# Four graph layers on one core: VectorE reads PSUM for one operand, two banks are held longer, and the order tables are replaced

## The reference

```python
x = _layernorm(x + _L0_gnn_ref(x, adj, ...))   # attention, 12 heads of 32, masked by adj, beta * adj added
x = _layernorm(x + _L1_gnn_ref(x, adj, ...))   # two digraph convolutions
x = _layernorm(x + _L2_gnn_ref(x, adj, ...))   # two more, with softmax of h h^T and triangles
x = _layernorm(x + _L3_gnn_ref(x, adj, ...))   # attention with adj as an added bias, output projection
```

```python
u_left = einsum('bih,bjh->bij', h, h @ W_left.T) / temper
u_right = einsum('bih,bjh->bij', h, h @ W_right.T) / temper
u = u_left * upper_triangle_with_diagonal(adj) + u_right * transposed(upper_triangle(adj))
d = exp(u) * adj
ctx = (d / (d.sum(axis=2) + 1e-10)) @ (h @ W_lin.T + b_lin)
h = relu((ctx - mean) / (std + 1e-3) * ln_a + ln_b)
```

## Time and profile before

| | |
|---|---|
| median of 3 executions | 2729.16 us (2726.61 to 2732.68) |
| the profiled execution | 2730.39 us, span 2728.5 us |
| PE busy | 2582.3 us, 95% |
| POOL busy | 2117.1 us, 78% |
| DVE busy | 2077.7 us, 76% |
| ACT busy | 2046.5 us, 75% |
| mean granted clock of TensorE | 0.986 of full speed |

### The profile page before, as it was taken

The page is one execution under the profiler, slowest core; times in us unless marked ns, Lnnn a source line. Parts: engine busy times, 40 slices in busy tenths (PEclk is TensorE's granted clock), DMA queues, the critical chain, the costliest instruction groups (busy, mean ns, idle before and its releaser), DMA issues.

```text
span 2728.5 us, 90881 instructions
## 1 busy us (share of the span) xinstructions
PE 2582.3 (95%) x33728; PEld 1930.4 (71%) x33728; DVE 2077.7 (76%) x7848; ACT 2046.5 (75%) x5716; POOL 2117.1 (78%) x3211
## 2 busy tenths in 40 slices
PE   5899999999999999999999999999999999999995
PEld 4667777776777777777777777777777777777763
DVE  6677877777877777777777777777787777887774
ACT  6667777777777777777777777777777777787775
POOL 6577878778778788778787788888787787887774
PEclk9899999999999999999999999999999999999997
DMA  7734544445444544444454454444454544454433
GB/s 182 164 62 78 90 86 83 91 84 93 81 87 80 91 91 80 90 91 80 87 94 80 88 93 80 90 91 79 88 94 84 86 88 79 85 96 82 78 61 74
DMA packets 809952, 243.18 MB, mean 89 GB/s; under 512 B 768688, under 2 KB 808752, under 8 KB 809520
## 3 DMA queue, kind: packets, MB, share of 16 engines
q1 hardware_dynamic: 801056, 222.42, 45.5%
q10 hardware_dynamic: 8464, 14.94, 1.8%
HBM read 35.92 MB, written 12.58 MB: 18 GB/s over the span
## 4 chain that ended last, share of the span: by engine, by line
PE 45%; POOL 18%; DVE 16%; ACT 7%; DMA 6%; issue 6%; SPq 1%; DVEq 0%; POOLq 0%; ACTq 0%
PE bank L921 7%; PE bank L923 6%; PE bank L922 6%; PE bank L912 5%; PE bank L913 5%; PE bank L914 5%; DMA region<-region 5%; POOL region L717 3%; DVE region L1091 3%; POOL ab L733 3%; PE bank L995 3%; ACT region L832 2%; POOL region L706 2%; PE bank L951 2%; POOL region L733 2%
## 5 line engine op out<-in xcount | busy, mean ns | idle before, releaser
L912 PE MATMUL bank<-region,w_hi 128*128 128x128 f16 x3960 | 686.0, 220 | 35.0 <-DMA region<-region 25.0
L913 PE MATMUL bank<-region,w_hi 128*128 128x128 f16 x3960 | 685.6, 220 | 0.0
L914 PE MATMUL bank<-region,w_lo 128*128 128x128 f16 x3960 | 685.4, 220 | 0.0
L921 PE MATMUL bank<-w_hi,region 128*128 128x384 f16 x1815 | 593.9, 327 | 11.4 <-DMA region<-region 6.1
L923 PE MATMUL bank<-w_hi,region 128*128 128x384 f16 x1815 | 593.2, 327 | 0.0
L922 PE MATMUL bank<-w_lo,region 128*128 128x384 f16 x1815 | 593.1, 327 | 0.0
L717 POOL TENSOR_TENSOR region<-region 128x512 f16<-128x512 f32 x330 | 385.2, 1167 | 220.6 <-ACT region L838 219.2
L832 ACT ACTIVATE region<-region,small 128x128 f32<-128x128 f32 x1320 | 419.8, 390 | 133.1 <-DVE small L1091 73.2
L912 PEld LDWEIGHTS bank<-region,w_hi 128*128 128x128 f16 x3960 | 390.0, 98 | 63.3 <-issue 26.4
L1091 DVE CUSTOM_DVE_ANT_0 region<-bank,mask 128x128 f32<-128x128 f32 x1320 | 304.4, 285 | 134.5 <-PE bank L951 123.2
L913 PEld LDWEIGHTS bank<-region,w_hi 128*128 128x128 f16 x3960 | 389.9, 98 | 23.8 <-issue 16.5
(11 more groups left out here) (229 smaller groups left out, 7795.8 us busy)
## 6 DMA issues: line engine op xcount, KB each, us to landing
region<-region SPq DMA_TRANSPOSE x715, 3.1
last_unit<-w_dram ACTq DMA_DIRECT2D x19, 576.0 KB, 6.0
x<-x_dram SPq DMA_DIRECT2D x55, 192.0 KB, 2.5
out_dram<-region SPq DMA_DIRECT2D x55, 192.0 KB, 2.2
adj<-adj_dram SPq DMA_DIRECT2D x55, 64.0 KB, 2.3
mask<-adj_t_dram SPq DMA_DIRECT2D x55, 64.0 KB, 2.0
rows<-rows_dram ACTq DMA_DIRECT2D x5, 576.0 KB, 4.3
last_unit<-last_unit SPq DMA_TRANSPOSE x117, 3.1
```

The lines of the kernel that those rows point to most:

```text
L912: pe.matmul(dst, lhsT=w_hi[:, w, k, cols], rhs=t_hi[u][:, k, :], start=(k == 0), stop=False)
L913: pe.matmul(dst, lhsT=w_hi[:, w, k, cols], rhs=t_lo[u][:, k, :], start=False, stop=False)
L914: last = pe.matmul(dst, lhsT=w_lo[:, w, k, cols], rhs=t_hi[u][:, k, :], start=False, stop=(k == DT - 1))
L921: pe.matmul(dst, lhsT=t_hi[u][:, k, :], rhs=w_hi[:, w, k, :], start=(k == 0), stop=False)
```

## The change

The arithmetic is the same, but for where intermediate values lie:

- `divide` writes the reciprocals into a free part of the bank of `attend` 2 (k = 0) or `attend` 5 (k = 1), and the division reads them there. For k = 0 the result also goes into that bank, over its first 384 columns, and `residual` 0 reads it there. For k = 1 the reciprocal comes first and the three small instructions after it; one of their results goes into the bank too.
- `READ_BY` names `residual` 0 as the last reader of `attend` 2's bank and `divide` 1 as that of `attend` 5's, in place of ACT's copy. PE's next product in that bank waits for them.
- `u_gcn` is three instructions of 128 columns in place of one of 256 and one of 128: left half times mask into SBUF, right half times mask into its own place in the bank, and the sum of the two. The denominator of the first two inner norms goes into the last column of `mix`'s bank.
- All wanted times of `PARTS`, all of `SHIFTED`, and `PERIOD` are new. The estimates are the same but for those shown, and so are the parts and what they follow.

```diff
-PERIOD = 20.1080
+PERIOD = 20.0000
 SHIFTED = {
-    0: (-214.647, -123.076, -82.970, -144.420, -205.803, -198.625, -397.860, -243.257),
-    1: (2.746, -8.453, 4.931, -1.139, 6.274, 8.107, -14.342, 6.813),
+    0: (-36.402, -56.825, -47.629, -24.020, -12.966, -30.610, -30.673, -21.116),
+    1: (-25.105, -7.955, -24.201, -25.096, -24.419, -21.463, -17.102, 0.286),
...
-    7: (-152.694, -18.243, -3.403, 0.458, 0.008, -0.828, -3.076, -0.403),
+    7: (7.020, 0.542, 0.535, 1.926, 0.328, -0.007, 2.628, -1.299),
...
-    15: (-1.918, 0.226, -15.546, 0.179, -0.256, 1.107, -162.141, 0.517),
+    15: (-62.686, 1.008, 1.008, 0.000, 0.000, 1.219, -1.236, 0.075),
...
 PARTS = {
-    (VECTOR, "u_gcn", 0): (-186.142, 0.656, 0.877, ((PE, "u_gcn", 0), (POOL, "sides", 0)), ()),
+    (VECTOR, "u_gcn", 0): (-238.867, 0.680, 0.800, ((PE, "u_gcn", 0), (POOL, "sides", 0)), ()),
-    (VECTOR, "residual", 0): (-132.856, 0.580, 0.750, ((VECTOR, "divide", 0), (POOL, "bias_x", 0)), ()),
+    (VECTOR, "residual", 0): (-148.149, 0.480, 0.620, ((VECTOR, "divide", 0), (POOL, "bias_x", 0)), ()),
-    (POOL, "residual", 0): (-202.457, 1.137, 1.220, ((SCALAR, "spread", 0),), ()),
+    (POOL, "residual", 0): (-154.722, 1.050, 1.150, ((SCALAR, "spread", 0),), ()),
-    (VECTOR, "centre", 2): (-204.301, 0.463, 0.560, ((SCALAR, "inner_spread", 2),), ()),
+    (VECTOR, "centre", 2): (-459.753, 0.525, 0.670, ((SCALAR, "inner_spread", 2),), ()),
...
-           "scores": lambda s: (VECTOR, "scores", s), "attend": lambda s: (SCALAR, "attend", s),
+           "scores": lambda s: (VECTOR, "scores", s), "attend": lambda s: {DT - 1: (VECTOR, "residual", 0), 2 * DT - 1: (VECTOR, "divide", 1)}.get(s, (SCALAR, "attend", s)),
...
             def divide(i, k):
                 u = i % UNITS
+                held = bank("attend", DT * k + DT - 1, i)
+                inverse = held[:, PD - 2 * H:PD - H]
+                dve.wait_ge(*max((scalar_done.at(i, "o", DT * k + t) for t in range(DT)), key=lambda at: at[1]))
+                dve.reciprocal(inverse, o_un[u][:, :, HD]).then_inc(numbers.of(i), 1)
                 if k:
+                    not_low = held[:, PD - H:PD]
                     dve.wait_ge(*topped.at(i, "low", 2 * DT - 1))
-                    dve.tensor_scalar(flag[u], low[u], 0.0, None, ALU.not_equal).then_inc(numbers.of(i), 1)
+                    dve.tensor_scalar(not_low, low[u], 0.0, None, ALU.not_equal).then_inc(numbers.of(i), 1)
                     dve.wait_ge(*numbers.at(i, "low is not 0", k))
-                    dve.scalar_tensor_tensor(flag[u], top[u], 0.0, flag[u], ALU.not_equal, ALU.max).then_inc(numbers.of(i), 1)
-
-                dve.wait_ge(*max((scalar_done.at(i, "o", DT * k + t) for t in range(DT)), key=lambda at: at[1]))
-                dve.reciprocal(inv[u], o_un[u][:, :, HD]).then_inc(numbers.of(i), 1)
-                if k:
-                    dve.wait_ge(*numbers.at(i, "inverse", k))
-                    dve.tensor_tensor(inv[u], inv[u], flag[u], ALU.mult).then_inc(numbers.of(i), 1)
+                    dve.scalar_tensor_tensor(flag[u], top[u], 0.0, not_low, ALU.not_equal, ALU.max).then_inc(numbers.of(i), 1)
+                    dve.wait_ge(*numbers.at(i, "row is not 0", k))
+                    dve.tensor_tensor(inverse, inverse, flag[u], ALU.mult).then_inc(numbers.of(i), 1)
                 dve.wait_ge(*numbers.at(i, "kept" if k else "inverse", k))
-                dve.tensor_tensor(o[u].rearrange("p (h c) -> p h c", c=HD), o_un[u][:, :, 0:HD],
-                                  inv[u].unsqueeze(2).broadcast_to([128, H, HD]), ALU.mult).then_inc(mixed_out.of(i), 1)
+                dst = o[u] if k else held[:, 0:D]
+                dve.tensor_tensor(dst.rearrange("p (h c) -> p h c", c=HD), o_un[u][:, :, 0:HD],
+                                  inverse.unsqueeze(2).broadcast_to([128, H, HD]), ALU.mult).then_inc(mixed_out.of(i), 1)
 
             def u_gcn(i, layer):
...
-                dve.tensor_tensor(u_pair[u], bank("u_gcn", layer, i)[:, 0:2 * N].rearrange("p (a n) -> p a n", n=N), mask_pair[u], ALU.mult)\
-                   .then_inc(numbers.of(i), 1)
-                dve.wait_ge(*numbers.at(i, "masked", layer))
-                dve.tensor_tensor(e_of(i, "u_gcn", layer), u_pair[u][:, 0, :], u_pair[u][:, 1, :], ALU.add).then_inc(mixed_out.of(i), 1)
+                left, right = (bank("u_gcn", layer, i)[:, n * N:(n + 1) * N] for n in range(2))
+                dve.tensor_tensor(u_left[u], left, mask_pair[u][:, 0, :], ALU.mult).then_inc(numbers.of(i), 1)
+                dve.tensor_tensor(right, right, mask_pair[u][:, 1, :], ALU.mult).then_inc(numbers.of(i), 1)
+                dve.wait_ge(*numbers.at(i, "right masked", layer))
+                dve.tensor_tensor(e_of(i, "u_gcn", layer), right, u_left[u], ALU.add).then_inc(mixed_out.of(i), 1)
...
-                dve.tensor_scalar(col(u, DENOM3), made[:, D:D + 1], 1e-10, 1e-3, ALU.add, ALU.mult).then_inc(numbers.of(i), 1)
+                dve.tensor_scalar(denom_of(made), made[:, D:D + 1], 1e-10, 1e-3, ALU.add, ALU.mult).then_inc(numbers.of(i), 1)
...
-                    dve.scalar_tensor_tensor(z[u], o[u], 1.0, x[u], ALU.mult, ALU.add, accum_out=col(u, SUM)).then_inc(mixed_out.of(i), 1)
+                    dve.scalar_tensor_tensor(z[u], bank("attend", DT - 1, i)[:, 0:D], 1.0, x[u], ALU.mult, ALU.add, accum_out=col(u, SUM)).then_inc(mixed_out.of(i), 1)
```

More of the change, by code:

```diff
@@ L171 @@
-    (SCALAR, "scores", 0): (-191.838, 1.860, 2.040, ((VECTOR, "scores", 0),), ()),
-    (PE, "scores", 2): (-190.896, 0.360, 0.610, ((SCALAR, "scores", 1),), ()),
-    (SCALAR, "attend", 3): (-190.869, 0.165, 0.450, ((PE, "attend", 3),), ()),
-    (SCALAR, "norm", 1): (-190.057, 0.599, 0.740, ((POOL, "residual", 1),), ()),
-    (PE, "mix", 0): (-188.893, 0.680, 0.900, ((POOL, "bias", 5), (VECTOR, "delta_gcn", 0)), ()),
-    (PE, "attend", 1): (-188.165, 0.330, 0.520, ((SYNC, "scores", 1),), ()),
@@ L253 @@
-    (VECTOR, "scores", 0): (12.131, 0.850, 0.420, ((PE, "scores", 0), (VECTOR, "masks", 0)), ()),
-    (VECTOR, "turn", 2): (18.250, 0.465, 0.743, ((SCALAR, "turn", 2),), ()),
-    (SYNC, "scores", 2): (44.537, 1.240, 4.000, ((POOL, "scores", 2), (PE, "attend", 1)), ()),
-    (SCALAR, "norm", 3): (45.613, 0.597, 0.740, ((POOL, "residual", 3),), ()),
-    (SYNC, "scores", 3): (47.973, 1.240, 4.000, ((POOL, "scores", 3),), ()),
-    (VECTOR, "gain", 1): (54.699, 0.916, 1.240, ((POOL, "inner", 1),), ()),
@@ new lines @@
+    (VECTOR, "add_bias", 1): (-670.136, 0.460, 0.720, ((PE, "project", 1),), ((SYNC, "store", 0),)),
+    (PE, "project", 0): (-637.670, 1.513, 1.710, ((SYNC, "turn", 0),), ()),
+    (VECTOR, "divide", 1): (-506.410, 1.223, 1.632, ((SCALAR, "attend", 3), (SCALAR, "attend", 4), (SCALAR, "attend", 5)), ()),
+    (SYNC, "scores", 5): (-484.398, 1.240, 4.000, ((POOL, "scores", 5), (PE, "attend", 4)), ()),
+    (SCALAR, "norm", 2): (-483.671, 0.598, 0.740, ((POOL, "residual", 2),), ()),
+    (VECTOR, "centre", 2): (-459.753, 0.525, 0.670, ((SCALAR, "inner_spread", 2),), ()),
@@ new lines @@
+    (POOL, "inner", 0): (-210.702, 0.520, 0.620, ((VECTOR, "inner", 0),), ()),
+    (VECTOR, "delta_gcn", 0): (-204.878, 0.201, 0.409, ((SCALAR, "u_gcn", 0),), ()),
+    (VECTOR, "add_bias", 17): (-200.635, 0.460, 0.720, ((PE, "project", 17),), ()),
+    (VECTOR, "gain", 2): (-199.552, 0.525, 0.810, ((POOL, "inner", 2), (VECTOR, "centre", 2)), ()),
+    (POOL, "low", 0): (-190.195, 0.880, 1.130, ((SCALAR, "project", 0),), ()),
+    (SYNC, "turn", 3): (-182.635, 1.240, 3.600, ((POOL, "turn", 3),), ()),
@@ new lines @@
+    (SCALAR, "project", 15): (-107.167, 0.371, 0.570, ((PE, "project", 15),), ()),
+    (PE, "mix", 1): (-106.849, 0.680, 0.900, ((POOL, "bias", 8), (VECTOR, "delta_gcn", 1)), ()),
+    (SYNC, "scores", 0): (-106.620, 1.240, 4.000, ((POOL, "scores", 0),), ()),
+    (VECTOR, "residual", 1): (-106.539, 0.480, 0.620, ((VECTOR, "gain", 1),), ()),
+    (SCALAR, "project", 7): (-104.296, 0.371, 0.570, ((PE, "project", 7),), ()),
+    (POOL, "bias", 5): (-104.031, 0.955, 1.090, ((SCALAR, "project", 5),), ()),
@@ new lines @@
+    (SYNC, "scores", 1): (-32.143, 1.240, 4.000, ((POOL, "scores", 1), (PE, "attend", 0)), ()),
+    (POOL, "bias", 13): (-28.491, 0.955, 1.090, ((SCALAR, "project", 13),), ()),
+    (PE, "project", 18): (-26.656, 1.466, 1.660, ((SYNC, "turn", 6),), ()),
+    (VECTOR, "project", 2): (-22.857, 0.464, 0.742, ((SCALAR, "project", 2),), ()),
+    (VECTOR, "project", 7): (-20.187, 0.463, 0.741, ((SCALAR, "project", 7),), ()),
+    (SCALAR, "norm", 3): (-19.901, 0.597, 0.740, ((POOL, "residual", 3),), ()),
@@ L286 @@
+    (SCALAR, "project", 17): (451.246, 0.420, 0.620, ((VECTOR, "add_bias", 17),), ()),
+    (VECTOR, "add_bias", 0): (467.275, 0.460, 0.720, ((PE, "project", 0),), ((SYNC, "store", 0),)),
 }
@@ L553, in inner_of, with denom_of @@
             return bank("mix", k, i)[:, 0:D]
+        def denom_of(made):
+            return made[:, PD - 1:PD]
         def across(tile):
```

343 lines of the change are left out of this document (166 added, 177 removed), and 52 rows, old and new, of the table SHIFTED.

## The result

| | before | after |
|---|---|---|
| median of 4 executions | 2730.61 us (2726.61 to 2732.68) | 2656.99 us (2654.54 to 2660.45) |
| the profiled execution | 2730.39 us, span 2728.5 | 2656.05 us, span 2654.3 |
| PE idle within the span | 146.2 us | 89.5 us |

The ratio is 0.9733 (0.9716 to 0.975): faster by 2.7%. The forecast was 2715 with a range down to 2680, so the direction was right and the gain of 73 us was five times the 15 forecast.

What follows compares the result with a forecast made beforehand. PE, busy 2582.3 of 2728.5 us, was taken as the bound, with its idle time the main thing to move. From 2730.4: -10 + 5.8 + 2 + 0.4 - 13.5 = 2715.1 us, range 2680 to 2750.

Steps and rivals of the forecast that it cites:

- What bounds the kernel: Whole span: PE busy 95%, so only its 146.2 us idle, its clock and the tail can move.
- Part 1: VectorE's lock waits on five lines: 78 us go, 15% reaches PE, -10 us, ends 0 and -28.
- Part 2: u_gcn as three instructions: chain 0.09 us longer, paid by each graph's first convolution, +5.8 us, ends 0 and +11.6.
- Part 3: Banks of attend 2 and 5 held 3.0 and 1.4 us longer: +2 us, ends 0 and +30.
- the second rival: PE waits for the longer-held banks, or products are placed worse: slower, 2745 us, chance 0.30.
- Part 4: Fourth layer's division: small instructions now behind the reciprocal, last graph's projection later, +0.4 us once.
- Part 5: New order of parts: less idle in 200 to 1000 us, fewer misplaced products, -13.5 us, ends +20 and -43.
- The rule that spoke against the change: VectorE sources: PSUM costs 62 fixed cycles more than SBUF, 37 us of VectorE, total 2725 us; left out of the sum.
- The first (relief never reaches PE): Rival on VectorE and PE: stalls go but PE's waiting pattern stays, 2729 us, chance 0.15.
- The third: Rival on the order: PE's 67 us middle idle halves and both ends gain 10, 2685 us, chance 0.17.
- PE's idle time in the middle falling far below 45 us: Sign of error for PE in 200 to 2550 us; idle above 67 us was the other.

Runs made afterwards that it cites:

- e2: The changed kernel's new VectorE instructions in the old order of parts, banks given out anew, three divisions kept in SBUF: 2674.26 us, ratio 0.9799.
- e9: e3 with only the fourth layer's division reading PSUM, first layer's division and residual as before: 2699.55 us, ratio 0.9888.
- e10: e5 with two added, unused VectorE instructions of 0.30 us each ahead of the fourth layer's division: 2693.70 us, ratio 0.9871.
- e6: e2 with the old divisions and first residual, so only u_gcn and the inner norms' denominators are new: 2717.42 us, ratio 0.9951.
- e3: The kernel before with only the banks of attend 2 and 5 held longer and given out anew, three excepted: 2728.29 us, ratio 0.9993.
- e7: e2 with each graph's masks moved later on VectorE, just ahead of its own add_bias 0: 2658.39 us, ratio 0.9741.
- e12: The kernel before with two edits, the fourth layer's division reading PSUM and masks moved later: 2684.57 us, ratio 0.9835.
- e5: e3 with the divisions and the first residual reading PSUM: 2689.18 us, ratio 0.9853.
- e11: The changed kernel with masks two places earlier on VectorE, ahead of add_bias 17 and u_gcn 0, in 54 graphs: 2677.69 us, ratio 0.9813.
- e8: The kernel before with only each graph's masks moved later on VectorE, just ahead of its own add_bias 0: 2706.74 us, ratio 0.9918.

## Why the prediction was right in direction and wrong in size

**What bounds the kernel.** Right that PE's idle time was what could move (it gave 56.7 us; 17.5 came from its busy time, which the prediction held fixed), wrong in how it was taken: as many short waits of separate causes, each priced by the row that ended it. They were the visible edge of one loop. The chain's 45% for PE stood on the page of before and was not read.

**Part 1 is the step that failed.** It had two factors. The first, VectorE's lost time, was right. Its busy time fell by 108.3 us, to 1969.4; `masks` account for 36 of it (89.8 us in all before, 54.2 after), for their new place; the added instruction of `u_gcn` cost 64 x 2 x 0.09 = 11.5; so 108.3 - 36 + 11.5 = 84 us against the 78 forecast. The second factor, that 15% of it reaches PE, is what failed. The same instructions in the old order gave 55 us (e2), not 10, above even the stated end of 28. That factor was built from waits of PE ended by VectorE, so it saw neither POOL's side of the lock (2117.1 to 2079.9 us busy; in e9 one division gave 29 us, and in e10 VectorE's own time at that place counted for an eighth) nor a delay that passes by way of ACT, POOL and the transpose, and is booked by the earlier trace rows as a wait on DMA. Its counts were off as well, without effect on the 15%: the five rows of VectorE have 27 + 12 + 5 + 10 + 2 = 56 waits, not 54, and the stretch holds 57 graphs of 41 PE parts, not 52 of 45.

The Trainium skill, page "SBUF — State Buffer", section "Who interferes with whom", says that a VectorE instruction with two SBUF inputs contends with a GpSimd instruction that reads SBUF, that the ports they share are an exclusive lock, and that the order of issue decides who blocks. The trace agrees in kind: at 1246.10 VectorE was first and lost nothing, and POOL lost 0.36 us. That is somewhat less than the 0.51 us that they overlapped.

**Part 2** was right in the length of the chain, not in that it is paid. The timeline of one first convolution after, start and length in us:

```profile
1501.13 0.28 DVE L1130 TENSOR_TENSOR region<-bank,region 128x128 f32<-128x128 f32 x1
1501.33 0.29 DVE L1131 TENSOR_TENSOR bank<-bank,region 128x128 f32<-128x128 f32 x1
1501.65 0.30 DVE L1133 TENSOR_TENSOR bank<-bank,region 128x128 f32<-128x128 f32 x1
...
1502.69 0.29 DVE L1138 TENSOR_TENSOR region<-bank,mask 128x128 f32<-128x128 f32 x1 [0.22 <-ACT bank L873]
...
1503.80 0.87 PE L1001 MATMUL bank<-region 128*128 128x386 f32 x2
```

1501.13 to 1501.95 is 0.82 us for 0.84 forecast. But the +5.8 us are not paid: `mix` starts 0.82 us after `delta_gcn` ends (1502.98), and 0.8 us is the usual room of a first convolution in the middle, so in the new order the chain has room here. In the old order the time fell with the three instructions too (e6, -13 us together with the denominators); there the stalls that went must have outweighed them.

**Part 3** was right, and the second rival fell with it: 0.9993 (0.9984 to 1.0002) in e3, and no wait of PE on the residual or the division after. **Part 4**, 0.4 us at the end, wasn't tried and is below what can be measured.

**Part 5** came near in size for another reason. The forecast was -13.5; on top of the new instructions the order is worth 17 us, on the old ones 32. The reason given, fewer misplaced products in the graphs with shifted times, is at most part of it: e7 has the old order but for `masks`, and equals after. What mattered in the middle was that `masks`, 0.57 us of work and 1.07 of lock stalls a graph, stood ahead of the scores' reader on the loop. Part 1 said of them only that they keep their own stalls.

**The rule that spoke against the change**, of the Trainium skill's page "VectorE: DVE Perf Modes", section on the TRN2 errata, would have made the total 2725 and is further from the result than the forecast. L1207 reads PSUM in 548 ns, where L1197 took 559 from SBUF; L1131 and L1133 take 290 and 300. The trace of after disagrees with it as that of before did.

**The rivals.** The first (relief never reaches PE) and the second fell. The third gave 2685 by halving PE's idle time in the middle; it fell there from 66.8 to 11.3 us (4.8, 0.7 and 5.8 of the three stretches), and both ends together gained 1.2 us, not 10. It came nearest, but it put 43 us of its gain down to the order and 10 to the instructions. The prediction named PE's idle time in the middle falling far below 45 us as a sign that it was wrong, and that is what came.

**What stays open.** What costs e12 its 26 us against e7 outside the middle and nothing inside it; how e9's 29 us divide between POOL's delay and the rest; whether the move of `masks` pays by their stalls or by their own work; which of the first layer's division and residual gives the 12 us between e9 and e5; and what of e11's loss is the wait for `adj` and what its place ahead of `u_gcn`. In the middle there is nothing left to gain by order: 999.29 of 1000 us are PE's work.

## What to carry to other kernels

Read the chain's shares beside the busy shares: an engine that was 95% busy but only 45% of the chain was paced here by a loop through others. A delay on that loop came back in every graph, on engines that were busy for three quarters of the time: in the middle, 0.62 us less on it in e9 went with 0.7 us less per graph. A stall from a shared resource has two sides; look for what an undisturbed instruction held up on the other engine, and then take one operand out of the shared memory or move the instruction off the loop; here they gave 29 and 23 us alone and 44 together, of 73. Once the periodic part has no idle time left, further edits of that kind add nothing in it.

## What the hardware showed that was not expected

- One 0.56 us instruction of VectorE with two arrays in SBUF stretched a 1.00 us addition of POOL to 1.36 us, at the same place in each graph of the middle. The edit that undid this one overlap, and the small stalls beside it, gave 29 us (e9), 1.1% of the kernel.
- `masks`, 128 columns between SBUF buffers, take 0.22 and 0.35 us alone and 0.66 and 0.99 in the mean of the old place, up to 1.2 and 1.3. Moving those two instructions, 4% of VectorE's busy time before, was worth 23 us (e8).
- VectorE's destination in PSUM costs 8 to 9 ns on 384 columns (L1122: 561 to 564 against 553 to 555 ns for its form that writes SBUF).
